# Four layers on one core: another order of weight preparation in the first MLP, the low half of the output weights on another engine, and another order where attention meets the last MLP

## The reference

```python
def _L0_attn_ref(...): ...   # a Mamba block: in-projection, convolution, selective scan over 256 steps, out-projection
def _L0_ffn_ref(x, gate_w, gate_s, up_w, up_s, down_w, down_s):      # first MLP, int32 weights, 512 -> 1376 -> 512
    gate = silu(einsum('bsd,fd->bsf', x, gate_w.astype(x.dtype)) * gate_s)
    up = einsum('bsd,fd->bsf', x, up_w.astype(x.dtype)) * up_s
    return einsum('bsd,fd->bsf', gate * up, down_w.astype(x.dtype)) * down_s
def _L1_attn_ref(hidden_states, Wq, Wkr, Wdk, Wupk, Wupv, Wo):       # causal attention, 32 heads of 128, 8 key heads
    q = rope(hidden_states @ Wq.T); k = ...; v = ...                 # k and v from a low-rank latent
    attn = softmax(where(causal, q @ k.T / sqrt(128), -1e9))
    return (attn @ v) @ Wo.T
def _L1_ffn_ref(hidden_states, w1, mean_w1, w2, mean_w2, w3, mean_w3):   # second MLP, 512 -> 1792 -> 512
    W = lambda w, base: base + mean(abs(w - base)) * sign(w - base)      # one coefficient for a whole matrix
    return einsum(silu(x @ W(w1, mean_w1).T) * (x @ W(w3, mean_w3).T), W(w2, mean_w2))
```

## Time and profile before

| | before |
|---|---|
| median of 3 runs | 1749.05 us (1748.15 to 1751.51) |
| the profiled execution | 1750.26 us |
| its span, first to last instruction | 1748.5 us |
| granted clock of TensorE, mean over the span | 0.978 |
| busy: PE, its weight loads, DVE, ACT, POOL | 93%, 79%, 64%, 51%, 46% |
| 16 DMA engines, share of the span | 15.5% |

### The profile page before, as it was taken

The page is one execution under the profiler, slowest core; times in us unless marked ns, Lnnn a source line. Parts: engine busy times, 40 slices in busy tenths (PEclk is TensorE's granted clock), DMA queues, the critical chain, the costliest instruction groups (busy, mean ns, idle before and its releaser), DMA issues. The chain is left out here.

```text
span 1748.5 us, 25644 instructions
## 1 busy us (share of the span) xinstructions
PE 1618.7 (93%) x8758; PEld 1379.1 (79%) x8758; DVE 1118.6 (64%) x1580; ACT 895.7 (51%) x1905; POOL 802.8 (46%) x458
## 2 busy tenths in 40 slices
PE   5995999999978799999979999999999998899998
PEld 3862899999967588778868988888888887788876
DVE  4327999999976223365527677676767768755422
ACT  2336888888754344335425554545445454533321
POOL 2212899999965363335213332333223333466343
PEclk9998999999989899999989999999999998999999
DMA  3201010102020573002100010000100012144100
GB/s 118 67 1 58 1 46 10 55 0 103 1 97 1 215 268 130 18 1 91 37 25 25 25 49 24 24 24 27 45 24 24 30 55 73 37 156 163 42 19 30
DMA packets 25195, 97.79 MB, mean 56 GB/s; under 512 B 3104, under 2 KB 3360, under 8 KB 22688
## 3 DMA queue, kind: packets, MB, share of 16 engines
q1 hardware_dynamic: 24976, 96.75, 15.5%
q10 hardware_dynamic: 144, 0.07, 0.0%
HBM read 94.57 MB, written 2.23 MB: 55 GB/s over the span
## 5 line engine op out<-in xcount | busy, mean ns | idle before, releaser
L863 POOL TENSOR_TENSOR scratch_s<-scratch_s,scan_cm 128x1024 f32<-128x1024 f32 x96 | 227.4, 2369 | 25.5 <-DVE scratch_s L1035 25.4
L1861 POOL TENSOR_TENSOR stretch_turned<-stretch_turned,res_const 128x1024 f32<-128x1024 f32 x32 | 77.4, 2419 | 226.5 <-ACT stretch_turned L1704 226.5
L1547 PE MATMUL psum<-opnd_xh,query_wqh 128*128 128x256 f32 x512 | 151.6, 296 | 1.9 <-PEq L94 1.9
L1129 PE MATMUL psum<-res_const,scratch_s 128*128 128x128 f32 x1088 | 144.7, 273 | 2.2 <-POOL scratch_s L863 2.2
L1547 PE MATMUL psum<-opnd_xl,query_wqh 128*128 128x256 f32 x512 | 145.7, 285 | 0.0
L1547 PE MATMUL psum<-opnd_xh,query_wql 128*128 128x256 f32 x512 | 145.7, 285 | 0.0
L1129 PEld LDWEIGHTS psum<-res_const,scratch_s 128*128 128x128 f32 x1088 | 128.7, 141 | 18.3 <-POOL scratch_s L863 2.4
L1712 ACT ACTIVATE stretch_pa<-psum,stretch_nm 128x128 f32<-128x128 f32 x128 | 45.2, 365 | 159.5 <-DVE stretch_nm L1966 159.5
L919 ACT ACTIVATE scratch_s<-ssm_dt,ssm_vec 128x255 f32 (+1 forms) x256 | 112.4, 500 | 11.0 <-DVE scratch_s L1035 8.4
L1123 PE MATMUL psum<-scan_diag,scratch_s 128*128 128x256 f32 x448 | 111.8, 385 | 6.7 <-ACT scratch_s L911 6.7
L1123 PE MATMUL psum<-diag_odd_diag,scratch_s 128*128 128x256 f32 x448 | 110.0, 380 | 0.0
(11 more groups left out here) (332 smaller groups left out, 4749.9 us busy)
## 6 DMA issues: line engine op xcount, KB each, us to landing
mi_dw<-in_dw SPq DMA_DIRECT2D x24, 448.0 KB, 7.0
mi_dm<-in_dm SPq DMA_DIRECT2D x24, 448.0 KB, 7.3
query_raw<-in_w_q SPq DMA_DIRECT2D x8, 1024.0 KB, 4.7
query_raw<-in_w_o SPq DMA_DIRECT2D x8, 1024.0 KB, 4.8
gu_raw<-in_w_gu SPq DMA_DIRECT2D x11, 512.0 KB, 4.8
mlpa_raw<-in_w_mlp SPq DMA_DIRECT2D x7, 768.0 KB, 4.4
mlpa_base<-in_b_mlp SPq DMA_DIRECT2D x7, 768.0 KB, 6.0
mlpb_raw<-in_w_mlp SPq DMA_DIRECT2D x7, 768.0 KB, 4.2
```

The costliest lines, as they stand in the source:

```text
L863: nc.gpsimd.tensor_tensor(slot[h][r], slot[h][r], weights(4 * h, 4), ALU.mult).then_inc(weighted_pool, 1)
L1129: mm = nc.tensor.matmul(ps_y[:, t * P:(t + 1) * P], part[:, t * P:(t + 1) * P], ident, start=start and t == 0, stop=stop and t == QT - 1, ...
L1547: mm = nc.tensor.matmul(ps_q[:, h * SEQ:(h + 1) * SEQ], w[:, k, h * HD:(h + 1) * HD], x[:, k, b * SEQ:(b + 1) * SEQ], start=(k == 0 and w ...
L1861: nc.gpsimd.tensor_tensor(heads(turned[:, :]), heads(turned[:, :]), over_heads(C_SIN, SEQ), ALU.mult).then_inc(q_sine, 1)
```

## The change

In the first MLP ACT makes the high half of tile f+2 right behind the activation of tile f, and the differences of step f come after it; DVE makes the low half of tile f+2 behind its product of tile f, and the low halves of the down weights come last. (`prepare(f+2)` waits for all products of tile f, since it writes the buffers from which they are read.) Before, tile f+1 was prepared at the head of step f, from f = 1 on, so behind the differences of step 0.

In attention the low half of the output weights is one instruction of 128x2048 on DVE, after `maxima` and ahead of `probabilities` in `body(g, 0)`; POOL's two are gone, `wo_lo` counts one a group, PE waits for it once, at the head of the group's first `output`, and SP accordingly.

At the seam: POOL's `difference(0)` waits for `q_done` of 30 (the next unit's rotation), its `difference(1)` for `normed` of all 32 units; ACT's `y_norm(2)` comes after both `oh`; DVE's `y_moments_of(1)`, `whole(1)`, `y_shift(1)` come after both `ol`; and DVE's `whole_down(0)` moves from ahead of `accumulate` and `probabilities` of the last unit to behind `x_moments_of(0)`.

```diff
             def step(f, s):                                      # widen_phase, ACT
-                if exists(f + 1, F) and not (isinstance(f, int) and f + 1 < done):
+                if exists(f + 1, F) and done == 0:
                     prepare(f + 1, 1 - s)
...
                     nc.scalar.activation(m[:, :], ps[s][0], ACT.Silu, scale=sc).then_inc(first_done, 1)
                     if diff is not None and done:
+                        if exists(f + 2, F):
+                            prepare(f + 2, s)
                         if exists(f, N_SUMS):
                             differences(f, s)
...
             def step(f, s):                                      # widen_phase, DVE
-                if kind == "int" and exists(f + 1, F) and not (isinstance(f, int) and f + 1 < done):
+                if kind == "int" and exists(f + 1, F) and done == 0:
                     int_lows(f + 1, 1 - s)
-                if diff is not None and isinstance(f, int) and f >= 7:
-                    for k in rows_at[f]:
-                        dve.wait_ge(next_hi, k + 1)
-                        nc.vector.tensor_tensor(next_wl[:, k, :], next_raw[:, k, :], f32(next_wh[:, k, :]), ALU.subtract).then_inc(next_lo, 1)
+                if diff is not None and isinstance(f, int) and f >= 7 and done == 0:
+                    next_lows(f)
...
                                                    sc, mid[s % len(mid)][:, :], ALU.mult, ALU.mult).then_inc(second_done, 1)
+                    if done and exists(f + 2, F):
+                        int_lows(f + 2, s)
+                    if done and diff is not None and isinstance(f, int) and f >= 7:
+                        next_lows(f)
...
-                    sp.wait_ge(wo_lo, 2 * g)                     # attention, SP
+                    sp.wait_ge(wo_lo, g)
...
-                    sp.wait_ge(wo_lo, 2 * GROUPS)
+                    sp.wait_ge(wo_lo, GROUPS)
...
                         pe.wait_ge(wo_hi, g + 1)                 # attention, PE, output
-                        pe.wait_ge(wo_lo, 2 * g + 1)
+                        pe.wait_ge(wo_lo, g + 1)
...
-                    if b == 0 and t == 0 and h == 2:
-                        pe.wait_ge(wo_lo, 2 * g + 2)
...
-                    if ending(g, b, BATCH - 1) and t == 0:       # ACT body
-                        y_norm(2)
+                if ending(g, b, BATCH - 1):
+                    y_norm(2)
...
-            def output_weights(g):                               # POOL
-                pool.wait_ge(wo_hi, g + 1)
-                pool.wait_ge(neg_max, g * BATCH + 2)
-                for h in (slice(0, 2), slice(2, HPG)):
-                    nc.gpsimd.tensor_tensor(wol[:, h, :], raw[:, :].rearrange("p (h c) -> p h c", h=HPG)[:, h, :],
-                                            f32(woh[:, h, :]), ALU.subtract).then_inc(wo_lo, 1)
...
-                if b == 0:
-                    output_weights(g)
                 if ending(g, b, 0):
+                    pool.wait_ge(q_done, g * BATCH + b + 2)
                     difference(0)
                 if ending(g, b, 2):
                     pool.wait_ge(q_done, U)
                     residual(0)
                     residual(1)
                     mlp_low(0)
+                    pool.wait_ge(normed, U)
                     difference(1)
...
+            def output_weights(g):                               # DVE
+                dve.wait_ge(wo_hi, g + 1)
+                nc.vector.tensor_tensor(flat(wol), raw[:, :], f32(flat(woh)), ALU.subtract).then_inc(wo_lo, 1)
...
                 if last:                                         # DVE body
                     x_shift(0)
-                    y_moments_of(1)
-                    whole(1)
-                    y_shift(1)
...
                     nc.vector.tensor_tensor(ol[t], x, f32(oh[t]), ALU.subtract).then_inc(o_lo, 1)
+                if last:
+                    y_moments_of(1)
+                    whole(1)
+                    y_shift(1)
                 if more(g, b):
                     maxima(*after(g, b))
+                if b == 0:
+                    output_weights(g)
...
                 if ending(g, b, 2):
-                    whole_down(0)
                     for t in range(QT):
                         accumulate(v, b, t)
                 if more(g, b):
                     probabilities(*after(g, b))
                 if ending(g, b, 2):
                     x_moments_of(0)
+                    whole_down(0)
```

4 lines of the change are left out of this document (added).

## The result

| | before | after |
|---|---|---|
| median of four runs each, side by side | 1750.1 us (1748.15 to 1751.51) | 1720.58 us (1719.18 to 1724.65) |
| ratio, 95% interval | | 0.9835 (0.9823 to 0.9846) |
| span of the profiled execution | 1748.5 us | 1722.9 us |
| mean granted clock | 0.978 | 0.977 |

The forecast was 1717.9, the range 1709 to 1728. The profiled execution of after (1724.65) is the slowest of its four, for a reason ahead of any changed line: in the scan phase the clock fell at another place (first row before, second row after; the columns are those of the earlier trace rows).

A forecast was written before the change was run, and what follows sets the result against it. TensorE was taken as the bound, busy 93%, so gains come only where it idles or runs at a low clock. 12.4 + 16.1 + 7.7 - 5.0 = 31.2 us, giving 1717.9, range 1709 to 1728.

The forecast's parts named there:

- First MLP: Tile 2's stall and low clock go; PE ends 14.3 us earlier, less a tail of 1.90: net 12.4, bounds 9.5 to 13.2.
- tile 3 is ready at 603.3, just in time: First MLP: DVE's low half, meeting POOL's step 1, ends at 603.3; PE needs tile 3 at 603.7.
- The tail of 1.9 us: End of the first MLP: low halves of the last three down rows stand behind DVE's last product, costing 1.90 us.
- Output weights: Attention: DVE's subtraction gives 2.3 us a group, 16.1 for g = 0 to 6, plus 7.7 in the last: 23.8.
- the hole: Attention: DVE's idle 3.53 us before the reciprocal at 1148.96, in which the 2.3 us subtraction fits.
- the 3.29 us of the last four scalings: Attention, unit b = 1: DVE's last four scalings take 3.29 us while POOL works on the output weights.
- The charge of 0.2 for a restart: Attention: 0.2 us taken off each group's 2.51 us gain for PE's restart at the output weights.
- Rival B: The new DVE instruction collides or takes twice 2.3 us; groups 0 to 6 gain nothing: 1734 us, 7%.
- Seam: New waits and order delay the chain of norm steps to PE's third token transpose: -5.0 us, bounds -9 and +1.
- `flips` 1.65 earlier: Seam: without `whole_down(0)` ahead of the last `probabilities`, the reciprocal moves to 1478.9 and flips come 1.65 us earlier, at 1481.1.
- ACT idle for nearly 6 us ahead of the sign: Seam: ACT waits for POOL's `difference(1)` from 1478.9 until 1484.6 before `difference_sign(1)`.
- PE idle ahead of the third transposes: Seam: PE idles 4 to 5 us before the third token transpose, which it gets 4.8 us later.

The follow-up runs named there:

- e1: The kernel before with only the first MLP's lines of the change: 1739.15 us, 10.8 less than before.
- e9: The changed kernel with tile 4's raw weights asked for behind the first pair of step 2's blocks in the first MLP: 1719.5 us.
- e8: The changed kernel with the low halves of the down rows of tiles 9 and 10 ahead of DVE's closing product: 1718.72 us.
- e2: The kernel before with only the low half of the output weights moved to DVE, without any line of the seam: 1727.85 us.
- e3: The changed kernel with DVE's output-weight subtraction done twice, only the second counted: 1747.06 us.
- e11: The changed kernel with DVE's output-weight subtraction in two halves and two waits of PE: 1716.59 us.
- e4: The changed kernel with the seam in the order of before; only the wait of `difference(0)` is kept: 1714.69 us.
- e5: The changed kernel without POOL's wait on `normed` ahead of `difference(1)`: 1717.54 us.
- e6: The changed kernel with row 1's moments, `whole(1)` and `y_shift(1)` ahead of `ol`, and `y_norm(2)` between the two `oh`: 1716.77 us.
- e7: The changed kernel with the edits of e5 and e6 together: 1714.51 us.
- e10: The kernel before without POOL's wait for the row maxima, so its two output-weight subtractions stay on POOL but end sooner: 1734.85 us.

## Why the prediction was right, point by point

- **First MLP: 12.4 predicted, 10.2 measured in the trace, 10.8 by e1.** The mechanism held: stall and low clock gone, eight tiles at full clock. From the phase's first matmul to the end of its last tile 13.0 us went instead of 14.3, for the step "tile 3 is ready at 603.3, just in time" failed: the prediction kept POOL's step 1 at its old time, but it starts 1.5 us later relative to PE and catches the whole of DVE's low half. Why it starts later is open (e9). The tail of 1.9 us came out at 1.88, as predicted, but the prediction left out its price in clock: the stretch up to L387 has 10.24 us against 9.33 before, 0.9 more, and e8 gets 0.8 of it back. The bounds 9.5 to 13.2 hold it.
- **Output weights: 23.8 predicted, 22.6 measured (22.5 between e1 and e2, 22.0 by e2's median).** 2.3 us for the instruction was 2.29; the hole held it. A group gave 2.16 against 2.3, the last one 7.5 against 7.7. The size was right, and the reason half right: the prediction put the 3.29 us of the last four scalings down to POOL's output weights. These ended at 1150.31, ahead of the scalings at 1150.90; e3 shows that POOL's sine held them, behind a first delay of 0.9. The charge of 0.2 for a restart was too small: e11 puts it at 0.4.
- **Rival B** was priced at the whole gain of seven groups, 16.1. e3 makes that case real: at full clock a group has 71.98 us, no less than before (71.8), and seven groups lose 16.3. The price left out the clock behind a stall of 2.54 us a group, 4.5 us in e3's trace.
- **Seam: -5.0 predicted, -4.6 measured in the trace.** `flips` 1.65 earlier (1.6 measured), `difference(1)` over 3.5 us behind the scalings (3.5), ACT idle for nearly 6 us ahead of the sign (5.75), `y_shift(1)` 14.0 us behind `flips` (13.99), PE idle ahead of the third transposes (5.21): every step as written. By medians the changed kernel is 5.9 behind e4; e5 and e6 show the two delays apart, e7 their sum.
- **Sum.** 10.2 + 22.6 - 4.6 = 28.2, and the 1.9 us of clock at the start of attention make 30.1 between the two traces, against 31.2 predicted; by medians 29.5. So the mechanisms gave some 3 us less than forecast, and that the total of the traces came within 1.1 is in part luck. The spans of the two profiled executions differ by 25.6 only, 4.5 having gone ahead of the first changed line.

## What to carry to other kernels

An instruction that is late by less than 1 us on a shared path can run into the next long step of the other engine and lose 2 us more: list what POOL starts just behind each short DVE step, and put slack there, before moving work between engines. Where a producer ends within 0.2 us of its consumer's turn, hand it over in two halves; the extra wait was free and the split gave 3 us in eight groups. And a wait that keeps two engines apart must be read along the whole chain behind it: here `difference(1)` had room before the scalings, and the wait only delayed a sign step that stands ahead of PE's operands.

## What was not expected of the hardware

- A DVE step on 128x8 elements, 0.17 us alone, took 1.79 beside POOL's 128x1024 subtractions (e10) and ended with them (1143.65 and 1143.63), so this small step was caught as fully as the large ones.
- Splitting one 128x2048 subtraction into two of 128x1024 cost 0.07 us on DVE (2.29 and 2.36) and took 0.37 us off PE at the handover.
- An idle time of TensorE of 5.03 us instead of 3.16 was followed by a granted clock of 0.75 instead of 0.82 over the next ten us: 0.8 us more on top of the 1.9.
- The granted clock in an unchanged phase moved by itself between executions (0.83 and 0.77 over the same 50 us), enough to shift everything behind it by 4.5 us. The same at the start of attention (0.79 and 0.86 over 24 us, 1.9 us) would have passed for a gain of the change, had e1's trace not been set beside it.
